# Routing tables by token tile: sixteen comparisons of 128 columns a row in place of one of 2048

## The reference, cut to what matters

```python
def route(x, routing_token, num_tokens, k_eff):
    s = jnp.einsum('bnd,rd->brn', x, routing_token)[:, 0]
    scores = coor_descent(s, k_eff)
    sel_scores, sel_idx = jax.lax.top_k(scores, num_tokens)
...
sq, iq = route(x, rt_q, NQ, min(NQ * FETCH_K, SEQ))
skv, ikv = route(x, rt_kv, NKV, min(NKV * FETCH_K, SEQ))
xq = x[batch_idx, iq]
xkv = x[batch_idx, ikv]
routed_out = heavy_attn(xq, xkv, skv, rms_g, w_q_h, w_kv_h, null_kv, w_out_h)
...
out = out.at[batch_idx, iq].set(routed_out)
```

## Time and profile before

| what | us |
|---|---|
| median of 3 runs | 4359.72 |
| lowest and highest | 4358.93, 4363.67 |
| the profiled execution | 4365.84 |
| its span in the profile | 4364.1 |

### The profile page before, as it was taken

The page is one execution under the profiler, slowest core; times in us unless marked ns, Lnnn a source line. Parts: engine busy times, 40 slices in busy tenths (PEclk is TensorE's granted clock), DMA queues, the critical chain, the costliest instruction groups (busy, mean ns, idle before and its releaser), DMA issues. The chain is left out here.

```text
span 4364.1 us, 91886 instructions
## 1 busy us (share of the span) xinstructions
PE 4095.8 (94%) x36800; PEld 3421.5 (78%) x36800; DVE 2892.0 (66%) x5104; ACT 1852.2 (42%) x4838; POOL 877.6 (20%) x661
## 2 busy tenths in 40 slices
PE   5788879999999999989999999869999999999999
PEld 5677757888888888878888888757777778777777
DVE  9888858776666766665555676665565655656555
ACT  7434324343434434344444333324454444544544
POOL 0222202222222222222222222211101101111111
PEclk9899979999999999999999999969999999999999
DMA  8589652222222222211121111121202202022020
GB/s 312 161 231 240 193 171 73 91 81 85 92 84 91 81 87 90 77 55 59 60 69 59 59 59 62 45 85 37 56 8 51 49 15 54 8 54 47 15 44 13
DMA packets 341353, 360.60 MB, mean 83 GB/s; under 512 B 23104, under 2 KB 237376, under 8 KB 340928
## 3 DMA queue, kind: packets, MB, share of 16 engines
q1 hardware_dynamic: 262592, 287.52, 22.0%
q0 software_dynamic: 12288, 33.56, 3.7%
q10 hardware_dynamic: 66048, 33.56, 2.9%
HBM read 228.21 MB, written 76.02 MB: 70 GB/s over the span
## 5 line engine op out<-in xcount | busy, mean ns | idle before, releaser
L1684 POOL TENSOR_TENSOR l_prob<-l_prob,l_inv 128x768 f32<-128x768 f32 x256 | 389.8, 1544 | 1692.5 <-DVE l_inv L1641 1692.5
L1235 ACT ACTIVATE l_prob<-l_ps_s,l_neg_max 128x192 f32<-128x192 f32 x1024 | 420.7, 443 | 7.6 <-DVE l_neg_max L1617 7.3
L2305 DVE TENSOR_REDUCE h_neg_max<-h_ps_s 128x1 f32<-128x1024 f32 x256 | 312.8, 1222 | 165.9 <-PE h_ps_s L2089 164.1
L2226 ACT ACTIVATE h_prob<-h_ps_s,h_neg_max 128x1024 f32<-128x1024 f32 x256 | 285.7, 1116 | 280.2 <-DVE h_neg_max L2308 280.2
L1617 DVE TENSOR_REDUCE l_neg_max<-l_ps_s 128x4 f32<-128x768 f32 x256 | 233.1, 952 | 238.3 <-PE l_ps_s L1004 219.3
L2101 PE MATMUL h_ps_t<-ident,h_prob 128*128 128x128 f32 x2048 | 272.9, 276 | 14.6 <-ACT h_prob L2226 14.1
L2101 PEld LDWEIGHTS h_ps_t<-ident,h_prob 128*128 128x128 f32 x2048 | 228.6, 141 | 62.5 <-issue 27.7
L2362 DVE COPY h_probs_t<-h_ps_t 128x512 f32<-128x512 f32 x256 | 176.9, 691 | 124.7 <-PE h_ps_t L2101 123.8
L2113 PEld LDWEIGHTS h_ps_o<-h_probs_t,ahead_then_values 128*64 128x64 f32 x4096 | 220.9, 137 | 43.5 <-issue 37.2
L2113 PE MATMUL h_ps_o<-h_probs_t,ahead_then_values 128*64 128x128 f32 x4096 | 251.8, 276 | 0.0
L1235 ACT ACTIVATION_READ_ACCUMULATOR l_prob<-l_ps_s,l_neg_max 128x1 f32 x1024 | 235.6, 230 | 0.0
(11 more groups left out here) (388 smaller groups left out, 10901.1 us busy)
## 6 DMA issues: line engine op xcount, KB each, us to landing
toep_back<-taps_padded ACTq DMA_DIRECT2D x32, 1024.0 KB, 10.3
x<-xg SPq DMA_DIRECT2D x64, 512.0 KB, 7.9
l_xin<-x SPq DMA_DIRECT2D x128, 256.0 KB, 3.3
l_xres<-x SPq DMA_DIRECT2D x128, 256.0 KB, 3.2
l_val_side<-l_val SPq DMA_DIRECT2D x256, 128.0 KB, 3.1
out_dram<-l_res SPq DMA_DIRECT2D x128, 256.0 KB, 2.0
ahead_then_values<-x SPq DMA_DIRECT2D x126, 256.0 KB, 3.1
xin<-in_L_attn_x_dram SPq DMA_DIRECT2D x32, 768.0 KB, 5.9
```

Of the source, the lines that this page charges most:

```text
L1235: last = nc.scalar.activation(prob[t % 2][:, h, pair, :], ps_s[:, h, pair, BOTH], ACT.Exp, bias=neg_max[:, t % 2, h, pair:pair + 1], accum ...
L1684: nc.gpsimd.tensor_tensor(mine, mine, spread(inv[:, t % 2, h, :], [1, PAIRS], [0, WIN + P]), ALU.mult).then_inc(p_normed, 1)
L2226: nc.scalar.activation(prob[i % 2][:, :].rearrange("p (a k) -> p a k", a=2), ps_s[i % 2][:, :, :], ACT.Exp, bias=neg_max[:, qt % 2, h:h + ...
L2305: nc.vector.tensor_reduce(at, ps_s[i % 2][:, :, :].rearrange("p a k -> p (a k)"), AX_X, ALU.max, negate=True).then_inc(max_step, 1)
```

## The change

`one_hot` is laid out by token tile: [128, 16, 128] in place of [128, 128, 16]. DVE fills it with 16 comparisons a row, one for each token tile: the numbers 0 to 127 in bf16 (`steps_b`, 128 columns) against one column of `column`, a [128, 1] operand in fp32. The stationary operand of the matmul is then `one_hot[:, t, :]`, 128 neighbouring elements. `steps_wide` and `column_b` with their two operations on ACT are gone, and a copy of 128 columns on ACT takes their place. `hot_made` is raised once a row, by the sixteenth comparison.

```diff
--- before.py
+++ after.py
@@ -1793,15 +1793,14 @@
         total_no = sb("r_total_no", [P, ROWS, HI])
         in_block = sb("r_in_block", [P, HI, COLS], BF16)
         what = sb("r_what", [P, PARTS, HI, COLS], BF16)
-        one_hot = [sb(f"r_one_hot{i}", [P, P, NCH], BF16) for i in range(2)]
-        steps_wide = sb("r_steps_wide", [P, P, NCH], BF16)
-        column_b = sb("r_column_b", [P, COLS], BF16)
+        one_hot = [sb(f"r_one_hot{i}", [P, NCH, P], BF16) for i in range(2)]
+        steps_b = sb("r_steps_b", [P, P], BF16)
         listed = sb("r_listed", [P, ROWS, PARTS, HI])
 
         ps_list = [ps(f"r_ps_list{i}", [P, 512]) for i in range(4)]
 
 
-        wide_made = sem("r_wide_made")
+        steps_made = sem("r_steps_made")
         made, what_made, dve, hot_made, list_made, list_kept = (
             sem("r_" + n) for n in "made what_made dve hot_made list_made list_kept".split())
         steps = keep["steps"]
@@ -1828,14 +1827,13 @@
                     if row >= 4:
                         pe.wait_ge(list_kept, row - 3)
                     for t in range(NCH):
-                        last = nc.tensor.matmul(ps_list[row % 4][:, 0:PARTS * HI], one_hot[row % 2][:, :, t],
+                        last = nc.tensor.matmul(ps_list[row % 4][:, 0:PARTS * HI], one_hot[row % 2][:, t, :],
                                                 what[:, :, :, row * NCH + t], start=(t == 0), stop=(t == NCH - 1))
                     last.then_inc(list_made, 1)
 
             @block.scalar
             def _(act):
-                nc.scalar.activation(column_b[:, :], column, ACT.Identity).then_inc(wide_made, 1)
-                nc.scalar.activation(steps_wide[:, :, :], spread(steps[:, 0:P], [1, P], [0, NCH]), ACT.Identity).then_inc(wide_made, 1)
+                nc.scalar.activation(steps_b[:, :], steps[:, 0:P], ACT.Identity).then_inc(steps_made, 1)
                 for row in range(ROWS):
                     if row < KC:
                         round_weights(act, row)
@@ -1861,13 +1859,16 @@
                     last = nc.vector.tensor_tensor(what[:, m, :, :], in_block[:, :, :],
                                                    spread(parts[:, :, m], [0, HI], [1, COLS]), ALU.mult)
                 last.then_inc(what_made, 1)
-                v.wait_ge(wide_made, 2)
+                v.wait_ge(steps_made, 1)
 
                 for row in range(ROWS):
                     if row >= 2:
                         v.wait_ge(list_made, row - 1)
-                    nc.vector.tensor_tensor(one_hot[row % 2][:, :, :], spread(column_b[:, row * NCH:(row + 1) * NCH], [0, P], [1, NCH]),
-                                            steps_wide[:, :, :], ALU.is_equal).then_inc(hot_made, 1)
+                    for t in range(NCH):
+                        at = row * NCH + t
+                        last = nc.vector.tensor_scalar(one_hot[row % 2][:, t, :], steps_b[:, :], column[:, at:at + 1], None,
+                                                       ALU.is_equal)
+                    last.then_inc(hot_made, 1)
                     if row >= ROWS - 2 * KC and row % 2 == 0:
                         step(part_weights(v, (row - ROWS) // 2 + KC))
                 v.wait_ge(list_kept, ROWS)
```

## The result

| | before | changed |
|---|---|---|
| median of 9 runs, us | 4361.24 | 4374.87 |
| lowest and highest | 4358.93, 4368.16 | 4371.74, 4382.69 |
| profiled execution, span | 4365.84, 4364.1 | 4377.99, 4376.3 |

The changed kernel takes 1.003 times as long (95% interval 1.0022 to 1.0039): 13.6 us between the medians, 10 to 17 us by the interval.

The account below looks back on a forecast made before the run. PE was taken to bound the routing stage at 2.55 us a row, DVE after the change: 51.1 + 0.23 + 2.55 + 0.22, together 54.1 against 42.36 us, +11.8 on 4359.72 gives 4371.5 us; own range 4368 to 4375.

Parts of the forecast that it names:

- The price of one comparison: DVE's small bf16 comparison with a [128, 1] operand: 0.134 us fixed plus 0.033 of data, 0.167 us.
- DVE becomes the bound by a hair in the first half: Routing rows: sixteen small comparisons take DVE 2.67 us a row, just above PE's 2.55.
- The roundings lie open: Second half of the rows: four groups of weight roundings on DVE, 8.4 us, no longer hidden under PE.
- The hand-over and PE's last row: End of the rows: 0.23 us comparison tail and semaphore, 2.55 PE's last row, 0.22 to `r_listed`.
- The weights' layout: PE's weight loads read adjacent columns: -0.84 us at best, 0 at worst; 0 taken.
- The clock: PE reaches full clock 4.0 us after dense work starts; half-rate stretch may change by 2 us either way; 0 taken.
- The first (operand hidden): DVE comparisons: operand cost hides behind the previous instruction, 0.117 us each, and PE gains; -1.9 us; chance 0.21.
- The second (no gain from bf16): DVE comparisons: sixteen-bit data brings nothing, 0.200 us each, 3.20 a row; +20.2 us; chance 0.12.
- The third: DVE comparisons run one column at a time, 0.27 us each, 4.3 us a row; +38 us; chance 0.04.
- The fourth: The change does not do what it says, for instance the comparisons merge; excluded by instruction order, no chance given.
- The total: Whole kernel: +11.8 us on a median of 4359.72, giving 4371.5 us, +0.27%.
- The estimate of 94 ns an instruction: DVE's small comparisons by the skill's formula: 1.5 us a row, total about as before; not adopted.

Follow-up runs that it names:

- run 3: Changed kernel plus five series of comparisons into an unread scratch tile: 0.163 us with the operand, 0.102 with a constant; row stretch 53.53 us again.
- run 4: Changed kernel with the compared steps in fp32 in place of bf16: 0.196 us a comparison, row stretch 61.35 us.
- run 6: Changed kernel with three buffers of one_hot in place of two: 2.60 us a row in the first half, row stretch 52.84 us.
- run 5: Changed kernel with DVE's weight roundings moved to POOL subtractions, ACT scaling the raw weights: row stretch 58.2 us, ratio to the kernel before 1.004.
- run 1: Changed kernel keeping the new layout, but one wide two-source comparison a row: pair 0.150 us, PE 2.40 us a row, row stretch 48.75 us.
- run 7: Kernel before with the matmul's 88 moving elements made neighbours: pair 0.073 us at half clock, row stretch 29.64 us, from 42.36.
- run 8: Changed kernel with the matmul's 88 moving elements made neighbours, so both operands are adjacent: pair 0.073 us, row stretch 51.59 us.
- run 2: Changed kernel with the old one_hot layout, each small comparison writing every sixteenth element: 0.28 us each, row stretch 83.4 us.

## Why the prediction was right

- **The price of one comparison.** Predicted 0.167 us from fp32 rows, half of the data's part, and the operand paid every time; measured 0.163 (run 3), 251 ns long in the rows. The halving for bf16 is shown by run 4 (0.196), the operand's 56 ns by run 3 (60 ns). The side on which the sum fell hung on little: by the prediction's own border, 0.155 us an instruction would have been too little to measure, 8 ns less than it is.
- **DVE becomes the bound by a hair in the first half.** Predicted 2.67 us a row, measured 2.68. The agreement hides two errors of opposite sign: DVE's own part is 2.61, and 0.07 a row comes from two buffers, which the prediction did not price (run 6). That the sum meets the row so closely is luck.
- **The roundings lie open.** Predicted 2 x 2.67 + 2.10 = 7.44 us for two rows, measured 7.31, which is 2 x 2.61 + 2.10: in the second half the buffers cost nothing. The term of 8.4 us was read from the earlier trace rows, and it is most of the 11.2 us. By the sum, the change would have cost 2 to 3 us without it, too little to measure; this is an estimate, as run 5, which was to show it, brought a new cost of its own.
- **The hand-over and PE's last row.** Predicted 2.55 us for the last row; it is 2.40 (run 1). The row stretch came out at 53.53, predicted 54.1: the comparisons and roundings up to the last row give 0.3 us of the difference, the hand-over and PE's last row the other 0.3. (The way to `r_listed` is 0.20 us by the prediction's own numbers, not 0.22.)
- **The weights' layout.** The prediction left about 50 ns a pair without a cause, allowed the stationary stride all of it, and took none, as the moving operand's stride stays. Runs 1, 7 and 8 settle it at half clock: 9 ns for the weights, 77 for the moving operand. Its floor of 0.107 us, 128 columns of weights at 0.83 ns, was wrong: a pair can take 0.073. The total doesn't feel it, since PE is not the bound. The Trainium skill's rule on 16-byte lines ("Advanced Engine Details and Errata", "SBUF Cachelines") holds for the moving operand, 0.150 against 0.073 us. For the stationary one these runs hardly bear it out: 9 ns with the moving operand strided, and with it adjacent, strided and adjacent weights both give 0.073 at half clock. The Trainium skill's "TensorE: Matmul & The Clock Gate", in "Weight-path perf modes", has a fast load that reads packed or strided columns; the two equal pairs agree with that as far as 0.073 us can show.
- **The clock.** Predicted no change with 2 us either way. In the 6.10 us from 2947.90 the mean granted clock is 0.74, which makes 3.2 us at 0.50 and the rest at 1.00. Before, the 4.00 us at 0.52 make 3.8 us at 0.50, so the prediction's 4.0 was a little long. The half-rate stretch is 0.6 to 0.7 us shorter, a gain of some 0.3 us.
- **The rivals.** The first (operand hidden) fell: it needed less than 0.155 us. The second (no gain from bf16) is run 4's number, not the changed kernel's. The third is about what the strided output of run 2 costs, but the new layout doesn't have it. The fourth was excluded by the order of instructions, and the 256 instructions are in the trace.
- **The total.** 11.8 us predicted, 11.2 measured in the row stretch, 13.6 between the medians. The median of 4374.87 lies 3.4 us over the forecast of 4371.5, just inside its range; 1.5 of them are the kernel before, whose median is 4361.24 over nine runs and was 4359.72 over three. The 2.4 us between 11.2 and 13.6 are not explained by any stage of the profiled executions; they are inside the interval, and the scatter of whole runs is larger. (A slip without weight: 4381, the upper end named with rival 2, is 1.1 us over that rival's 4379.9, not half a microsecond.)

The estimate of 94 ns an instruction by the Trainium skill's formula ("VectorE: DVE Perf Modes", "The TRN2 errata") roughly fits the form with a constant (0.102 us), not the one with a [128, 1] operand that the change uses. Had the sum gone by it, the forecast would have been no change.

## What to carry to other kernels

Price a split by the distance from start to start of the small instruction, its operand included, before counting what its data gains: here the data got twice as fast and DVE's row 2.3 times as long (1.13 to 2.61 us). An engine with 50% of its time free has no such room where other work is queued in it; take the slack for each half of a stage, in microseconds a row, and see what sits in it. When a matmul pair costs more than its columns, look at the stride of both operands, each by itself, and the moving one first.

## What the runs showed of the hardware that I had not expected

- A one-source comparison of 128 bf16 columns that writes every sixteenth element takes 0.28 us from start to start, against 0.163 with adjacent output and 0.196 with an fp32 input (runs 2, 3 and 4). Its records are 491 to 1119 ns long, so instructions overlap there more than in any other series.
- Moving operand 512 bytes apart: 0.150 us a pair for 88 columns at 1.2 GHz; adjacent: 0.073. The strided weights add 9 ns to the first and nothing that shows to the second (changed kernel, runs 1, 7 and 8).
- In run 7, with the moving operand adjacent and a wide comparison every 1.3 us, PE's granted clock rose to its full rate within the rows (1.00 from 2895.5 to 2899, in the lines below). In the kernel before, with the strided operand, it stayed at 0.50 for 41 us of back-to-back matmuls, and in the changed kernel too. In run 7 it was at 0.50 again in the second half, where PE was busy 7.29 of 12.80 us and waited for DVE.

Busy time by stretch of run 7, columns as in the earlier trace rows:

```profile
2895.50:2899.00 3.50, 3.30 (x49) 3.08 (x48) 3.17 (x4) 1.74 (x6) 0.00 (x0) 1.00 0.00 0
...
2904.50:2917.30 12.80, 7.29 (x91) 6.56 (x88) 11.24 (x13) 1.22 (x5) 0.00 (x0) 0.50 0.01 1
```

- While POOL subtracted from SBUF, single comparisons of DVE took up to 1365 ns in place of 250, and POOL's 15.0 us cost DVE some 13 us by the estimate of run 5.
